# A recommendation tower whose third layer gives one row of results per tile instead of one column

## The reference

```
e = stack([tbl_f[ids[:, f]] for f in range(26)], axis=1)
combined = concatenate([e, r_dense_x[:, None, :]], axis=1)
interact = einsum('bfd,bgd->bfg', combined, combined)
z = interact[:, triu_i, triu_j]                    # 351 per sample
h = concatenate([z, r_dense_x], axis=1)            # 479
h = maximum(h @ W_top1 + b_top1, 0)                # 512
h = maximum(h @ W_top2 + b_top2, 0)                # 256
y = h @ W_top3                                     # 1 per sample
```

## Time and profile before

| | before |
|---|---|
| median of 3 runs | 109.2 us (109.17 to 109.23) |
| profiled execution | 109.18 us |
| its span | 107.4 us |
| TensorE (PE) busy | 98.5 us, 92% |
| VectorE (DVE) busy | 79.8 us, 74% |
| ScalarE (ACT) busy | 75.0 us, 70% |
| GpSimd (POOL) busy | 66.3 us, 62% |
| granted TensorE clock, mean | 0.999 |

### The profile page before, as it was taken

The page is one execution under the profiler, slowest core; times in us unless marked ns, Lnnn a source line. Parts: engine busy times, 40 slices in busy tenths (PEclk is TensorE's granted clock), DMA queues, the critical chain, the costliest instruction groups (busy, mean ns, idle before and its releaser), DMA issues.

```text
span 107.4 us, 2605 instructions
## 1 busy us (share of the span) xinstructions
PE 98.5 (92%) x998; PEld 79.0 (74%) x998; DVE 79.8 (74%) x162; ACT 75.0 (70%) x149; POOL 66.3 (62%) x72
## 2 busy tenths in 40 slices
PE   5999899989799999999798978999999989998992
PEld 1356676657467675887478958999999979997991
DVE  6599999999999999999943974588338922685120
ACT  4499999999999999999706842475527732474430
POOL 3777777777777787777877777777777750000000
PEclk9999999999999999999999999999999999999999
DMA  3852749995663636621211221221121220000000
GB/s 46 334 209 58 235 76 372 374 345 113 217 197 101 221 78 218 225 92 49 55 49 49 53 50 49 63 66 49 49 55 49 58 67 3 6 0 0 6 0 1
DMA packets 5200, 11.64 MB, mean 108 GB/s; under 512 B 1979, under 2 KB 2491, under 8 KB 5189
## 3 DMA queue, kind: packets, MB, share of 16 engines
q1 hardware_dynamic: 3120, 7.27, 21.2%
q0 software_dynamic: 2048, 4.20, 14.2%
q10 hardware_dynamic: 20, 0.02, 0.1%
HBM read 11.48 MB, written 0.00 MB: 107 GB/s over the span
## 4 chain that ended last, share of the span: by engine, by line
DVE 46%; PE 44%; issue 6%; ACT 2%; POOL 0%; DVEq 0%; POOLq 0%
DVE onehot L464 22%; PE gram_ps L613 13%; DVE low L476 13%; PE top_ps L678 5%; PE tr_ps L594 5%; PE act_ps L667 4%; PE dve_ps L667 4%; DVE onehot L470 3%; DVE xt L473 2%; PE gram_ps L578 2%; PE top_ps L702 2%; PE tr_ps L653 1%; DVE xt L450 1%; PE dve_ps L626 1%; PE act_ps L626 1%
## 5 line engine op out<-in xcount | busy, mean ns | idle before, releaser
L287 POOL DMA_INDIRECT rows<-table,ids_sb x64 | 65.5, 1023 | 20.8 <-issue 19.2
L578 PE MATMUL gram_ps<-onehot,high 128*128 128x512 f32 x82 | 23.1, 410 | 1.9 <-DVE onehot L464 1.6
L578 PE MATMUL gram_ps<-onehot,low 128*128 128x512 f32 x82 | 22.1, 411 | 0.0
L578 PEld LDWEIGHTS gram_ps<-onehot,high 128*128 128x128 f32 x82 | 14.3, 188 | 8.8 <-DVE onehot L464 5.0
L578 PEld LDWEIGHTS gram_ps<-onehot,low 128*128 128x128 f32 x82 | 15.4, 189 | 3.9
L464 DVE TENSOR_TENSOR onehot<-dve_ps,row_f 128x1024 fp32r<-128x1024 f32 (+1 forms) x10 | 14.4, 1479 | 1.2 <-PE act_ps L554 1.2
L464 DVE TENSOR_TENSOR onehot<-gram_ps,row_f 128x1536 fp32r<-128x1536 f32 (+1 forms) x10 | 14.9, 1531 | 0.0
L613 PE MATMUL gram_ps<-xt 128*58 128x52 f32 x512 | 14.5, 217 | 0.3 <-issue 0.3
L483 DVE COPY gram_sb<-gram_ps 26x208 f32<-26x208 f32 x32 | 12.0, 376 | 3.6 <-PE gram_ps L613 2.4
L613 PEld LDWEIGHTS gram_ps<-xt 128*58 128x58 f32 x512 | 14.0, 133 | 0.9 <-issue 0.5
L385 ACT ACTIVATE onehot<-onehot 128x1344 fp32r<-128x1344 f32 (+1 forms) x10 | 14.3, 1426 | 0.0
(11 more groups left out here) (83 smaller groups left out, 111.7 us busy)
## 6 DMA issues: line engine op xcount, KB each, us to landing
table<-table SPq DMA_DIRECT2D x9, 512.0 KB, 3.6
rows<-table,ids_sb POOLq DMA_INDIRECT x64, 2.9
w1p_sb<-w_pairs SPq DMA_DIRECT2D x1, 768.0 KB
table<-table SPq DMA_DIRECT2D x1, 640.0 KB, 3.8
w_sb<-w SPq DMA_DIRECT2D x1, 512.0 KB
dense_sb<-dense SPq DMA_DIRECT2D x1, 256.0 KB, 5.1
w1d_sb<-w_dense SPq DMA_DIRECT2D x1, 256.0 KB
ids_sb<-ids SPq DMA_DIRECT2D x1, 52.0 KB, 2.0
```

Source lines behind the costliest of these rows:

```text
L287: pool.indirect_dma_start(rows[:, t, s - 1, :], None, tables[f], bass.IndirectOffsetOnAxis(ids_sb[:, t, f:f + 1], 0)).then_inc(gathered[t] ...
L578: last = pe.matmul(pick_ps[b][:], weights[:, c, :], onehot[:, b, c, :], start=(c == 0 and part == 0), stop=(c == CHUNKS[o] - 1 and part == 1))
```

## The change

The operands of the third layer's matmul change places: w3's column becomes the stationary operand and h2 the moving one, so that the result is one partition with 128 columns. y_ps and y_sb change their shape to that, and ScalarE copies 128 elements of one partition per tile. Tile t now holds the samples 128 t to 128 t + 127, which makes a tile's results one contiguous piece of 512 bytes of y. The host lays out ids and dense so that each partition still reads one contiguous piece, and orders ids_by_field, the indices of the one-hot fields, in the same manner. SP stores in two transfers: the first three tiles when the third y is there, the last tile when the fourth is.

```diff
-        y_sb = sb("y_sb", [P, TILES])
+        y_sb = sb("y_sb", [1, TILES, P])
...
-        y_ps = top_ps[:, 2, 0:1]
+        y_ps = top_ps[0:1, 2, :]
...
-            sp.dma_start(ids_sb[:], ids.rearrange("(p t) f -> p t f", t=TILES)).then_inc(ids_in, 16)
+            sp.dma_start(ids_sb[:], ids).then_inc(ids_in, 16)
...
-                    sp.dma_start(dense_sb[:], dense.rearrange("(p t) d -> p t d", t=TILES)).then_inc(dense_in, 16)
+                    sp.dma_start(dense_sb[:], dense).then_inc(dense_in, 16)
...
-            sp.wait_ge(y_out, TILES)
-            sp.dma_start(out.rearrange("(p t) o -> p (t o)", t=TILES), y_sb[:]).then_inc(stored, 16)
-            sp.wait_ge(stored, 16)
+            rows_out = out.rearrange("(t p) o -> o t p", t=TILES)
+            for done in (slice(0, TILES - 1), slice(TILES - 1, TILES)):
+                sp.wait_ge(y_out, done.stop)
+                sp.dma_start(rows_out[:, done], y_sb[:, done]).then_inc(stored, 16)
+            sp.wait_ge(stored, 2 * 16)
...
                 act.wait_ge(y_ready, n)
-                act.activation(y_sb[:, bass.ds(n - 1, 1)], y_ps, ACT.Copy).then_inc(y_out, 1)
+                row = y_sb[:, n - 1, :] if isinstance(n, int) else y_sb[:, bass.ds(n - 1, 1), :].rearrange("o t p -> o (t p)")
+                act.activation(row, y_ps, ACT.Copy).then_inc(y_out, 1)
...
-                    last = pe.matmul(y_ps, h2[:, c, :], w3_sb[:, c:c + 1], start=(c == 0),
+                    last = pe.matmul(y_ps, w3_sb[:, c:c + 1], h2[:, c, :], start=(c == 0),
                                      stop=(c == N2 // P - 1))
...
-        "dense": a["r_dense_x"],
-        "ids": a["ids"],
+        "dense": np.ascontiguousarray(a["r_dense_x"].reshape(TILES, P, D).transpose(1, 0, 2)),
+        "ids": np.ascontiguousarray(a["ids"].reshape(TILES, P, N_FIELDS).transpose(1, 0, 2)),
...
-            a["ids"].reshape(Q, G, TILES, N_FIELDS).transpose(3, 2, 1, 0).reshape(N_FIELDS, B)[ONEHOT]),
+            a["ids"].reshape(TILES, Q, G, N_FIELDS).transpose(3, 0, 2, 1).reshape(N_FIELDS, B)[ONEHOT]),
```

## The result

The changed kernel takes 109.60 us (109.58 to 109.61, six runs) against 109.19 of the kernel before: ratio 1.0037, interval 1.0025 to 1.005. It is slower, by 0.41 us; 109.09 was forecast, with a range up to 109.48. The profiled execution took 109.60 us with a span of 107.8.

The account below looks back on a forecast made before the run. The prediction took VectorE to bound the kernel until about 54 us, then TensorE, with the last copy and store uncovered. Copy +0.11, last matmul +0.02, waiting group -0.09, store -0.15: sum -0.11, forecast 109.09 us, range 108.75 to 109.48.

Parts of the forecast that it names:

- The dense groups: Third-layer matmuls at 76.35 and 102.27: a stream limit of 0.11 us per pass replaces an equal load limit, change 0.
- upper end of +0.11: Worst case per dense third-layer group: a first weight load that is not shortened, +0.11 us.
- The group behind a wait: Third-layer group at 87.55, waiting for ScalarE: one-column load and hidden L667 load bring its end forward, -0.09 us.
- The end: Last third-layer matmul, +0.02 us (0.40 to 0.41, with rounding), and the copy after it, +0.11 us.
- Three copies hidden: ScalarE's first three y copies, +0.11 us each, are covered by its waits for TensorE: 0.
- The store: Last store of y: few packets instead of 144 shrink the packet time from 0.20 to about 0.05 us, -0.15.
- Only the middle depends on the number of pieces: Last store: of 0.84 us to first packet, 0.20 of packets and 0.36 to landing, only the 0.20 shrinks.
- the 1.1: Sign at the last store: the prediction is wrong if its landing takes under 1.1 us (or over 1.58).
- Rival 4: Last store: the single row lands late, up to 2.0 us after issue, giving 109.84 us, slower; chance 0.16.
- Rival 3: Third-layer matmuls: passes fall from 0.111 to 0.058 us, giving 108.34 us, faster; chance 0.06.
- Rival 2: Last store: small writes also hold up the receipt, so one piece sheds 0.18 us more, 108.91 us; chance 0.16.
- Rival 1: Last store: row is cut up anyway or packet count never mattered, so -0.15 becomes 0, 109.24 us; chance 0.10.

Follow-up runs that it names:

- w96: Changed kernel with w3's column padded with zeros and 96 columns of it loaded in every tile's third layer; 109.03 us, ratio 0.9985 to the kernel before.
- mixed: Kernel before, with only the last tile's third layer and store in the new row form, the other tiles stored early in 12-byte pieces; 108.96 us, ratio 0.9979.
- one_store: Changed kernel with a single store of all four rows (2 KB) after the last copy; 109.67 us, ratio 1.0046 to the kernel before.
- w96_last1: Changed kernel with zero-padded w3, 96 columns loaded for tiles 0 to 2 and one column for the last tile; 108.93 us, ratio 0.9978 to the kernel before.

## Why the prediction was wrong

**The dense groups: the step that failed.** "So one limit of 0.11 replaces another: 0 at 76.35 and 102.27." The passes inside a group do keep their 0.11: four MATMULs span 0.60 with a last one of 0.27 in the group at 102.58, (0.60 - 0.27) / 3. What the step left out is the two borders. It took for granted that a load hides behind the stream ahead of it whatever the two loads' widths, and the runs show that it doesn't hold between 128 columns and 64 or fewer. Each such change of width inside a dense stream puts 0.20 us between two starts instead of 0.11, and on the way back the first load of 128 columns stands in the open besides. Measured +0.27 and +0.28, above even the upper end of +0.11.

The Trainium skill (TensorEngine Tiling (Array Packing), section Tiling Modes) has a rule that fits: the array can be divided by columns into parts of 32 or 64, and changing that division drains the engine. The stops at 64 columns and their absence at 96 agree; the page gives no price, and the runs here give about 0.28 us for going there and back. That a load of few columns changes the division by itself is an inference from these runs: they show where the stop comes and what it costs, not what the array does in it.

**The group behind a wait.** Forecast -0.09, "with its load hidden behind the fourth": measured +0.08. The entry is free there, since TensorE is waiting for ScalarE, the exit is not: the load of 128 columns at 88.37 has 0.22 us of idle time ahead of it. In w96 the chain reads

```profile
87.61 0.68 PE top_ps L707 x4
88.29 0.67 PE act_ps L672 x6
```

1.35 with its followers, 0.04 less than before: so much of the gain exists where no stop is paid.

**The end.** +0.02 forecast for the matmul (its own terms, 0.41 against 0.40, give +0.01), -0.01 measured; +0.11 for the copy, +0.10 measured. Three copies hidden: right; in the middle no new wait appeared.

**The store.** Forecast -0.15, measured -0.33. The packets did what the forecast said of them: 0.20 to 0.03, -0.17. "Only the middle depends on the number of pieces" was wrong: the time until the first packet, held at 0.84, fell by 0.11, and that behind the last packet by 0.05. The landing of 1.09 is just under the 1.1 that the prediction had named as a sign of being wrong. The shorter issue of SP explains little of the earlier first packet, since in mixed and one_store the issue takes 0.32 and the first packet still comes 0.75 behind its start; the cause stays open. Rival 4, a single row that lands late, was wrong in sign.

**The sum.** Terms measured: 0.63 - 0.01 + 0.10 - 0.33 = 0.39, and 0.02 by which the first group starts later: 0.41, the whole difference. The range was set by the rivals, and the only one of them that made the kernel slower was the store's. The upper end of +0.11 per group stood beside the zero, but even at two groups it would have left the time inside the range, and it was a load that isn't shortened, not a stop at a border.

**The rivals.** Rival 3 (streams at half the time) falls with the spacing of 0.11. The 56 ns that the prediction takes from the Trainium skill (TensorE: Matmul & The Clock Gate, section Back-to-back issue gap) stand there for a matmul by itself; for a stream of loads and matmuls that section gives about 81, and these fp32 passes measured 111. Rival 2 had a true core in the wrong place: the receipt of pieces of 4 bytes took 6 us, while those of 16 bytes gave 0.05 of the 0.18 that it priced. Rival 1 falls with the two packets and the -0.33.

## What to carry to other kernels

Where an operand swap makes the weights narrow, count the borders to the neighbouring matmuls as well as the passes: a dense fp32 stream that goes from 128 columns to 64 or fewer and back lost about 0.28 us each time, and padding the weights with zeros to 96 columns took that away. Put a narrow matmul where TensorE waits anyway, as w96_last1 and mixed do ahead of the last result. A result that goes out as one row is worth a longer copy when the store is the last thing on the chain (0.24 us net here).

## What the runs showed that was not expected

A store of 128 pieces of 4 bytes landed 7.3 us after its issue, whereas 128 pieces of 12 bytes took 1.8 and of 16 bytes 1.4, all with 144 packets from 128 partitions. Whether the cause is in memory or on the way there no run here tells.

The price stood in the trace before: behind the pair products, with weights of 58 columns, the chain reads

```profile
71.55 1.02 PE tr_ps L594 x8
```

0.13 more than eight passes of 0.111. On the way in, from 128 columns to 58, the last MATMUL of L667 starts at 79.31 and the first of L613 at 79.51: 0.205 us, as in the changed kernel from 128 columns to one (0.204). The semaphore that this load waits for had been up since 78.78. So the stop could be read from the kernel before, at a neighbour of the matmul that was to become narrow. No run took it away there.
